# A drain of TensorE raises the count of summed pairs

## What is computed

```
# first                                   # second
h    = layernorm(x) @ W                   msg  = w[:, None] * xn[src]
agg  = segment_sum(w[:, None] * h[src],   aggr = segment_sum(msg, dst) + (1 + eps) * xn
                   dst)                   h    = relu(relu(aggr @ W1 + b1) @ W2 + b2)
x   += relu(batchnorm(agg + bias))        x   += rownorm(h)
```

## Time and profile before

| | us |
|---|---|
| median of the three runs | 3905.8 |
| span of the profiled execution, first to last instruction | 3891.6 |
| first aggregation, gathers and sums | about 370 to 1558 |
| second aggregation | about 1950 to 3155 |
| TensorE busy, weight loads, VectorE, ScalarE, GpSimd (shares of the span) | 68%, 58%, 66%, 26%, 56% |

### The profile page before, as it was taken

How to read it: one execution, slowest core, us unless ns; L and a number is a source line. 1 busy time by engine, 2 the same in 40 slices (tenths; PEclk the granted TensorE clock), 3 DMA queues, 4 the chain that set the end, 5 groups by cost and what they waited for, 6 DMA issues and landing times. The chain is left out here.

```text
span 3891.6 us, 55224 instructions
## 1 busy us (share of the span) xinstructions
PE 2650.3 (68%) x15016; PEld 2238.8 (58%) x15016; DVE 2586.9 (66%) x6599; ACT 1024.1 (26%) x2120; POOL 2179.1 (56%) x2145
## 2 busy tenths in 40 slices
PE   6886555444454545789946666666666657999998
PEld 4666343333343434689935444444444537999998
DVE  8997655444554555976746566666666677888886
ACT  0021000000000000567501111111111127888886
POOL 1434566666666664335456666666666603666665
PEclk8998777777777777899967777777887768999999
DMA  3011333333333332000133333333333334776775
GB/s 90 4 46 58 102 91 92 91 91 88 91 92 88 92 88 63 12 1 23 55 90 96 96 96 96 96 96 94 98 95 94 95 103 165 216 216 212 213 215 146
DMA packets 164219, 387.69 MB, mean 100 GB/s; under 512 B 46324, under 2 KB 95528, under 8 KB 150561
## 3 DMA queue, kind: packets, MB, share of 16 engines
q0 software_dynamic: 99072, 233.49, 22.0%
q1 hardware_dynamic: 64929, 151.65, 11.4%
HBM read 342.69 MB, written 42.97 MB: 99 GB/s over the span
## 5 line engine op out<-in xcount | busy, mean ns | idle before, releaser
L1089 POOL DMA_INDIRECT g_got<-table,e_source x1568 | 1493.5, 952 | 845.0 <-issue 440.0
L1115 DVE TENSOR_TENSOR A<-A,psum 128x256 f32 x1664 | 698.6, 420 | 876.3 <-remote 532.0
L1182 PE MATMUL psum<-g_got,g_route 128*128 x3328 | 1034.7, 473 | 141.0 <-DMA g_got<-table,e_source 74.2
L1182 PEld LDWEIGHTS psum<-g_got,g_route 128*128 128x128 f32 x3328 | 771.9, 241 | 329.0 <-issue 198.4
L786 PE MATMUL psum<-ident,g_rows 128*128 128x128 f32 x208 | 63.0, 401 | 663.3 <-ACT A L834 410.2
L1098 DVE TENSOR_SCALAR g_route<-columns,e_local,e_weight 128x128 f32<-128x128 f32 x1664 | 471.6, 362 | 17.4 <-issue 12.2
L786 PEld LDWEIGHTS psum<-ident,g_rows 128*128 128x128 f32 x208 | 29.7, 190 | 703.8 <-ACT A L834 505.7
L834 ACT COPY A<-psum 128x256 f32 x52 | 19.3, 372 | 999.4 <-issue 637.4
L369 POOL DMA_INDIRECT records<-rec,place x120 | 120.6, 1005 | 233.7 <-ACT rec L585 159.1
L140 PE MATMUL psum<-e_xt_hi,e_w_hi 128*128 128x256 f32 x832 | 238.2, 286 | 5.4 <-issue 5.2
L1612 POOL TENSOR_TENSOR f_ht_lo<-f_ht,f_ht_hi 128x512 fp32r<-128x512 f32 x100 | 134.2, 1347 | 181.1 <-ACT f_ht_hi L1551 174.6
(11 more groups left out here) (413 smaller groups left out, 5403.5 us busy)
## 6 DMA issues: line engine op xcount, KB each, us to landing
e_w<-in_m_w SPq DMA_DIRECT2D x104, 1024.0 KB, 5.1
g_got<-table,e_source POOLq DMA_INDIRECT x1568
expert_table<-g_normal SPq DMA_DIRECT2D x52, 128.0 KB
table<-xn SPq DMA_DIRECT2D x49, 128.0 KB
X<-in_x SPq DMA_DIRECT2D x1, 6144.0 KB
table<-f_ring SPq DMA_DIRECT2D x24, 256.0 KB, 2.1
out<-X SPq DMA_DIRECT2D x1, 6144.0 KB
f_w<-in_f_w SPq DMA_DIRECT2D x2, 1024.0 KB, 6.5
```

What stands on the lines that cost most here:

```text
L1089: pool.indirect_dma_start(got[:, c % RING, :], None, rows, bass.IndirectOffsetOnAxis(ap=source[:, c:c + 1].bitcast(U32), axis=0)).then_inc ...
L1115: dve.tensor_tensor(to, to, sums_of(c), ALU.add).then_inc(added, 1)
L1182: ins = pe.matmul(sums_of(c), route[:, c % (GB + GSEM), :], row(got, at[j % GSEM]), start=True, stop=True)
```

## The change

Behind each group of four products TensorE drains (waits until its own earlier work is done), and the drain raises `pairs_summed` by two. The products raise nothing any more. The waits on `pairs_summed` in POOL and DVE stay as they are, so the count now moves in steps of two. There are 208 such drains in each aggregation, 416 in all.

```
                                 if c % 2 == 0 and c >= 2 * BANKS:
                                     pe.wait_ge(added, c - 2 * BANKS + 3)
-                                ins = pe.matmul(sums_of(c), route[:, c % (GB + GSEM), :], row(got, at[j % GSEM]), start=True, stop=True)
-                                if c % 2 == 1:
-                                    ins.then_inc(pairs_summed, 1)
+                                pe.matmul(sums_of(c), route[:, c % (GB + GSEM), :], row(got, at[j % GSEM]), start=True, stop=True)
+                            pe.drain().then_inc(pairs_summed, GSEM // 2)
                             if through_mlp and n >= 2 and g == 0:
                                 tiles_of.second_product(pe, n - 2)
```

## The result

The changed kernel takes 4036.96 us (median of four runs, 4029.91 to 4042.54), the kernel before 3903.78 us in the runs beside it (3891.8 to 3909.08): ratio 1.0338, interval [1.0314, 1.0362], some 132 us slower. The time lies inside the predicted range, near its upper end; the likeliest case (3912) missed it by 125 us. The ratios of this document leave out two slow executions, one of 5873 us of the kernel before and one of 4306 us of the second pacing kernel.

The account below looks back on a forecast made before the run. GpSimd's gathers at 1.25 us plus its waits for late counts were taken to bound the aggregations; terms 0 + 6 + 0 = +6 us gave 3905.8 to 3912 us, with a range of 3660 to 4040.

Parts of the forecast that it names:

- the likeliest case: Late counts stay late and TensorE's drains are hidden: 3912 us, own range 3893 to 3935, chance 0.42 including drains costing nothing.
- rival C: GpSimd's runs shorten from 16 to 12 gathers as drain counts come later: +108 us, 4014; chance 0.31 with exposed serial time.
- exposed time on TensorE: TensorE's serial work at the 416 drains, about 1.0 us each, not hidden by its waits: up to +416 us.
- wrong in any case: Sign against the whole forecast: drains of many us, VectorE and GpSimd both waiting for TensorE while its passes are few.
- the reading of the hold: In the aggregations, products are done but counts arrive some 8 us later, seemingly held while GpSimd works off 16 gathers.
- 0.93 us, say 1.0 with the drain itself: TensorE behind each drain: preparation 0.52 us plus slower first pass 0.41; nearly all hidden by its waits, six groups charged +6 us.
- The step of two, taken as 0: A group's first pair is told with its second, delaying two gathers 1.0 to 1.7 us; bounds 0 to +167 us, taken 0.
- the term for what waits behind the drain: On TensorE only tile products queue past a group; even if drains cannot end, the cycle stays 23.2 us: 0.
- Rival B: The drain's count is not held, so GpSimd's waits for sums shrink: 135 to 288 us faster, 3620 to 3770; chance 0.27.

Follow-up runs that it names:

- the second pacing kernel: Kernel before, no TensorE drains; GpSimd waits ahead of both halves of gather group q until its group q-2 has landed: ratio 0.9999.
- the paused kernels: Kernel before and changed kernel with a GpSimd drain ahead of every second gather (ratios 1.3807, 1.3786) or every eighth (1.1482, 1.1486).
- the run made for this: Kernel before with a GpSimd drain ahead of every eighth gather, 196 in all: 4028.6 us, ratio 1.1482.

## Why the prediction was right or wrong

**The range was met by its width.** The sum said +6 us and the measurement says 132. That the time lies in the range is luck as far as the likeliest case goes: the upper part of the range stood there for rival C and exposed time on TensorE, and of both only a part came about (below). What the prediction named as wrong in any case did come: drains of many us (up to 21.3), with VectorE (788.6 us) and GpSimd (522.4 us) waiting for TensorE's sequencer.

**What bounds the kernel, and the reading of the hold: right.** Counts arrive late, mostly with the ends of GpSimd's runs, and not because a product is late. Pauses in GpSimd's stream took all late counts away on the same chip.

**"0.93 us, say 1.0 with the drain itself", hidden: right in the sum.** A drain that isn't held costs nothing that can be measured (0.9985 as a ratio for 416 of them on the first chip and 1.0006 on the third, both with pauses in GpSimd's stream; 1.0005 for 104 without pauses), which fits the slack that the prediction names.

**The step of two, taken as 0: nearly right.** It measures 1.0015 alone, 6 us, of bounds that went up to 167; beside the drains it may be more.

**The step that failed.** It is the term for what waits behind the drain, taken as 0: "nothing else of TensorE is queued past a group except the tile products, and those wait for ScalarE". In the trace before L899 followed group 0 at 2500.46 with no idle time before it. The prediction went on to weigh the right mechanism: "if the drain itself cannot end while an earlier product's increment is held", groups 0 and 1 run after the release, "group 0 follows within 3 us and group 1 within 6", "GpSimd still is fed for its run. So a cycle of 23.2 us either way." The drain indeed can't end, but it holds up everything behind it, not the groups of sums only. In the second aggregation L899, L900 and L989 stand between group 0 and group 1. In the step shown they run after the release: 2559.25 to 2563.27, and then group 1's eight passes, 3.76 us at the lower clock. Group 1's count comes 7.87 us after the release where GpSimd has 5.0 us of work and the prediction had 3 us for a group. I had counted the passes of the groups and left out the 4.0 us of products between them, and had put the quick length of eight passes (1.99 us) into the sum and not the slow one. Where these products stand is said in the section on the kernel before, and a slow group is in the earlier trace rows, 3.43 us. So the cycle is 25.69 us in that step and not 23.2. By what share the drain brings this about, and by what share L893's late operand does, is open: the drains alone are shown to cost 109 us on their chip, those behind group 0 of the second aggregation 30, and the 105 us of the second aggregation are argued from the step.

The first aggregation bears the prediction out better. The drain behind group 2 is held there, L815 waits 7.77 us for it, and runs of 12 replace a part of those of 16; the step costs little more per gather:

```profile
714.38 2.05 PE L815 MATMUL psum<-g_xt,g_w 128*128 128x128 f32 x8 [7.77 <-issue]
714.96 0.95 POOL L1089 DMA_INDIRECT g_got<-table,e_source  x1 [2.83 <-PEq L1183]
...
732.67 0.95 POOL L1089 DMA_INDIRECT g_got<-table,e_source  x1 [2.96 <-PEq L1183]
```

17.71 us for 12 gathers is 1.476 us each, against 23.23 / 16 = 1.452: 19 us over 784 gathers, of the 27 measured.

**Rival C: the size nearly right, its mechanism in part.** It forecast runs of 12 instead of 16 and 4014 us. Runs did become 12, in the first aggregation; but in the second, which has the loss, it is 12 and 4: the number of standstills went from 104 to 163, where C had 131, and they are shorter, 2.97 to 2.99 us in the median instead of 3.47 to 3.57. Nor was the drain's later count the main reason: with counts told by the products as before, some 109 of the 132 us are lost. What C lacked was a TensorE that stands still at the drain.

**Rival B: fell.** The drain's count comes late too, and the stream with it. The rule that the prediction drew on for it, the sequencer's own push in the Trainium skill (Perfetto Trace Analysis, Per-engine timelines), may be right, but the push comes only once the drain ends. The Trainium skill (PSUM — Partial Sum Buffer, Engine vs sequencer instructions) says that a drain waits until the engine is fully idle; the runs agree, if an engine with a held completion isn't idle: the drain ends 0.02 us after the last pass where nothing is held, and up to 17.9 us after it where something is. The Trainium skill's rule in that section, that an engine's increment fires at completion, agrees with the third chip and the paused kernels, and disagrees with the earlier trace rows, where the increment comes 8 us after the end of the last pass.

**What stays open.** Why completions are held on some chips and not on the third was not found. The traces give one hint. Each of the 1568 gathers raises its semaphore 16 times, 25,088 updates in all. Of these the trace before has 3928, the trace after 5610, and every other run with late completions between 3943 and 5835; the two kernels with GpSimd's drains every two gathers have 22,833 and 23,722 on the same chip, and the four runs on the third chip at least 25,067. So late completions go with traces that miss most of the updates. Whether the recording of the trace takes part in the hold, or both have one cause, no run tests. Open is also how long a run of gathers may be before it happens, as the run made for this fell on the third chip. The changed kernel itself wasn't run there. The run with drains behind groups 2 and 3 and the pair with GpSimd's drains bound what 104 and 416 drains cost without a hold (5 and 2.6 us), but the former covers a quarter of the drains, and the latter has pauses that the changed kernel hasn't; that the change would be free on the third chip is argued, not shown.

## What to carry to other kernels

Before a drain or any other full stop goes into an engine's stream, look whether that engine's counts already arrive later than its work: where they do, the stop lasts as long as they are late, and all that could have run in the meantime, the side work between the groups above all, is laid behind the release. Ask too whether that side work's own inputs are late, or the stop gets the blame for a wait that is there without it. A wait whose releaser is "remote" or unexplained, and whose end keeps the same distance from another engine's last instruction, points at a held message. Here more synchronization on the side whose messages were late made it worse (1.0338), and pauses in GpSimd's stream cost more than they won (1.3807). Run the kernel on more than one chip before tuning against such a wait: one chip of three didn't have it, and was 10% faster.

## What the runs showed of the hardware

- Completions of TensorE come late while GpSimd issues indirect gathers back to back, on two chips and in the first traces; in the trace after most (75 of 126 late drains) come through 2.1 to 3.0 us after the run's last gather, some (19) in the middle of a run. With pauses of 2.7 us every two gathers none is held (no drain over 3.4 us). On a third chip none is held at all, in runs of 784 gathers without a standstill, and the kernel before takes 3508 us instead of some 3904.
- A drain of TensorE ends 0.02 to 0.05 us after the last pass where nothing is held, and costs next to nothing where its engine has slack (416 drains: 0.9985 and 1.0006; 104: 1.0005); where a completion is held it lasted up to 21.3 us with its products.
- A drain of GpSimd behind two gathers takes 3.9 us in the median and leaves a gap of 2.7 us; behind eight, 8.7 us with a gap of 3.0.
- GpSimd's gather takes 0.95 us and 0.30 us of issue on every chip; 784 of them take 985 us at best.
- The same products of TensorE took 4.0 us at a granted clock of 1.00 and 7.8 us at 0.50, after 9 us in which it did nothing.
